# Two heads on the two halves of TensorE, and the causal mask inside VectorE's maximum

## What is computed

```python
q, k, v = (heads(wq, bq), heads(wk, bk), heads(wv, bv))      # 16 heads of 8
q, k = _apply_rope(q, cos, sin), _apply_rope(k, cos, sin)
att = jnp.einsum('bhtd,bhsd->bhts', q, k) * scale
att = jax.nn.softmax(jnp.where(causal, att, -inf), axis=-1)
y = jnp.einsum('bhts,bhsd->bhtd', att, v)
...
scores = jnp.einsum('bhid,bhjd->bhij', q * scale, k)          # the mixture, 8 heads of 64
probs = jax.nn.softmax(scores, axis=-1)
```

## The kernel before

| slot | pass 1 | pass 2 | values of |
|---|---|---|---|
| 6, 7 | A groups 0, 1 | F groups 2, 3 | F groups 1, 2 |
| 0, 1 | A groups 2, 3 | A groups 0, 1 | F group 3, A group 0 |
| 2, 3 | F groups 0, 1 | A groups 2, 3 | A groups 1, 2 |
| 4, 5 | F groups 2, 3 | F groups 0, 1 | A group 3, F group 0 |

## Time and profile before

### The profile page before, as it was taken

One profiled execution on the slowest core, in us unless ns is written; L12 is line 12 of the kernel. 1 busy time (PEld: TensorE's weight loads), 2 busy tenths in 40 slices (PEclk: granted clock), 3 DMA queues, 4 the chain that ended last, 5 costly groups with the idle time before them and its releaser, 6 DMA issues.

```text
span 2072.6 us, 32651 instructions
## 1 busy us (share of the span) xinstructions
PE 1816.3 (88%) x11328; PEld 881.0 (43%) x11328; DVE 1580.1 (76%) x2934; ACT 1273.3 (61%) x2803; POOL 1047.0 (51%) x1124
## 2 busy tenths in 40 slices
PE   1658999989999898989999998999999899998775
PEld 0223443535444353535444453544435354443332
DVE  4538787888878788788888888887878888787461
ACT  0335757576675757566675756667575766758461
POOL 1223556363645646374655636465563636455433
PEclk8879999999999999999999999999999999999986
DMA  3231203112121302113120211213021121200000
GB/s 97 48 36 32 37 29 43 35 26 30 37 37 42 36 30 33 23 37 36 42 37 30 40 33 27 33 39 37 29 44 35 26 29 37 36 17 14 11 1 6
DMA packets 87617, 68.71 MB, mean 33 GB/s; under 512 B 10720, under 2 KB 83104, under 8 KB 87328
## 3 DMA queue, kind: packets, MB, share of 16 engines
q1 hardware_dynamic: 87456, 66.62, 17.5%
HBM read 32.51 MB, written 10.49 MB: 21 GB/s over the span
## 4 chain that ended last, share of the span: by engine, by line
PE 64%; DVE 13%; ACT 10%; POOL 6%; DMA 3%; issue 3%; SPq 0%; POOLq 0%; DVEq 0%; ACTq 0%; PEldq 0%
PE Y L463 11%; PE M L556 5%; POOL Z L1069 5%; PE S2a L428 5%; ACT Pq L683 5%; PE S1c L404 5%; PE S2b L428 4%; DVE nmaxF L848 4%; PE M L593 3%; PE S1b L404 3%; PE M L514 3%; PE M L489 3%; DMA Ks<-parts 3%; DVE ztmp L930 3%; PE Y L454 2%
## 5 line engine op out<-in xcount | busy, mean ns | idle before, releaser
L1069 POOL TENSOR_TENSOR Z<-Z,ztmp 128x1280 f32<-128x1280 f32 x112 | 324.5, 2897 | 327.9 <-DVE ztmp L958 326.8
L1036 POOL TENSOR_SCALAR_AFFINE_SELECT PT<-PT 128x256 f32<-128x256 f32 (+1 forms) x640 | 254.5, 409 | 386.6 <-ACT PT L668 383.5
L1060 POOL TENSOR_TENSOR Vf<-Vf,ztmp 128x512 f32<-128x512 f32 x256 | 349.0, 1363 | 102.2 <-DVE ztmp L930 93.6
L668 ACT ACTIVATE PT<-S2a 128x512 f32<-128x512 f32 x320 | 191.6, 599 | 170.6 <-PE S2a L422 166.2
L463 PE MATMUL Y<-PT,Vf 128*64 128x512 f32 x1024 | 274.8, 617 | 0.0
L672 ACT ACTIVATE PT<-S2a 128x512 f32<-128x512 f32 x256 | 153.6, 600 | 158.5 <-PE S2a L428 155.7
L930 DVE TENSOR_TENSOR ztmp<-xv,wv_s 128x512 f32<-128x512 f32 x256 | 238.0, 930 | 2.8 <-POOL Z L1069 2.8
L404 PE MATMUL S1c<-Kf,Qf 64*128 64x512 f32 x352 | 203.6, 659 | 36.2 <-ACT Pq L683 32.2
L404 PE MATMUL S1a<-Kf,Qf 64*128 64x512 f32 x352 | 204.5, 662 | 20.6 <-ACT Pq L683 20.6
L668 ACT ACTIVATE PT<-S2b 128x512 f32<-128x512 f32 x320 | 191.5, 598 | 26.3 <-PE S2b L422 26.0
L404 PE MATMUL S1b<-Kf,Qf 64*128 64x512 f32 x320 | 182.8, 652 | 9.5 <-ACT Pq L683 9.5
(11 more groups left out here) (108 smaller groups left out, 3760.7 us busy)
## 6 DMA issues: line engine op xcount, KB each, us to landing
Qs<-parts SPq DMA_DIRECT2D x96, 128.0 KB
Ks<-parts SPq DMA_DIRECT2D x96, 128.0 KB
tab_s<-in_tab SPq DMA_DIRECT2D x16, 512.0 KB, 4.5
xr<-out_x SPq DMA_DIRECT2D x32, 256.0 KB, 2.9
out_x<-res SPq DMA_DIRECT2D x32, 256.0 KB, 2.2
wa_s<-in_wa SPq DMA_DIRECT2D x16, 320.0 KB, 3.1
xl<-out_x SPq DMA_DIRECT2D x16, 256.0 KB, 3.0
out_x<-in_x SPq DMA_DIRECT2D x8, 256.0 KB, 4.4
```

The lines of the kernel that those rows point to most:

```text
L668: nc.scalar.activation(PT[:, slot % 2, b, :], t[:, :], ACT.Exp, scale=SCALE_A).then_inc(exps_done.sem, 1)
L1036: last = nc.gpsimd.affine_select(out=v, in_=v, compare_op=ALU.is_ge, fill=0.0, base=0, pattern=pattern, channel_multiplier=-1)
L1060: nc.gpsimd.tensor_tensor(Vf[:, i, :, :], Vf[:, i, :, :], vtmp[:, n % VBUF, :, :], ALU.add).then_inc(v_acc.sem, 1)
L1069: nc.gpsimd.tensor_tensor(Z[:, :, :, :], Z[:, :, :, :], ztmp[:, hh % 2, :, :, :], ALU.add).then_inc(z_acc.sem, 1)
```

## The change

1. **Layout.** Qs and Ks are [128, 8, 512] in place of [98, 16, 512]: even heads lie in rows 0 to 63, odd heads in rows 64 to 127. A head's contraction takes 48 rows (`ROWS_P1`) and, with the two rows of maxima, 50. (The 48 rows are the six products of parts; the zero rows are left out.) The weights' columns and the tables are laid out on the host so that even heads come out in partitions 0 to 63.
2. **Pairs.** The banks are ordered so that bank b (b even) and bank b+1 hold the same segments of an even head and its odd neighbour. Pass 1 and pass 2 issue both banks at once, at even steps; the first waits until both banks are free. Of both, all matmuls of the even head come first in the program, then those of the odd one.
3. **Mask.** The 16 mask matmuls of a group are gone. VectorE takes each maximum by `tensor_tensor_reduce`: the PSUM segment plus `maskw` (zeros, and -1e30 above the diagonal in its last 128 columns), written back in place, with the maximum in an accumulator. Each of the 16 segments has its own instruction, and each becomes two on the engine: the pass over the segment, and one that writes the accumulator out.
4. **Around it.** Split and negation of the maxima are two small instructions as before. The spreading DMAs are 24 of 64 KB in place of 12 of 128 KB; the rows of maxima go as two DMAs, of two rows each. The memsets at the start cover 2048 words in place of 4096 for Qs and Ks.

```diff
-    ROWS_P1 = 96
+    ROWS_P1 = NSP * DA
     ROWS_P2 = ROWS_P1 + 2
+    HALF = 64
...
+    for h0 in range(0, GA, 2):
+        BANKS_A1 += [[(h, 3, 0)] for h in (h0, h0 + 1)] + [[(h, 2, 0), (h, 0, 384)] for h in (h0, h0 + 1)]
+        BANKS_A2 += [[(h, 0, 0)] for h in (h0, h0 + 1)] + [[(h, 1, 0), (h, 3, 384)] for h in (h0, h0 + 1)]
+    BANKS_A1 += [[(h, 1, 0), (h + 2, 1, 256)] for h in (0, 1)]
+    BANKS_A2 += [[(h, 2, 0), (h + 2, 2, 256)] for h in (0, 1)]
...
                         for r in range(NSP):
-                            sp.dma_start(dst[DA * r:DA * r + DA, :, :],
-                                         parts[:, qk, order[r], :]).then_inc(scattered.sem, 16)
+                            for lo in (0, HALF):
+                                sp.dma_start(dst[lo + DA * r:lo + DA * r + DA, :, :],
+                                             parts[lo:lo + HALF, qk, order[r], :]).then_inc(scattered.sem, 16)
...
-                    pe.wait_ge(*s1_free(j, (n if group < SA else n + 1) - len(S1)))
+                    pe.wait_ge(*s1_free(j, n + 1 - len(S1)))
                     if group < SA:
-                        for h, qt, col in BANKS_A1[b]:
-                            hh, keys = GA * group + h, (qt + 1) * P
-                            nc.tensor.matmul(t[:, col:col + keys], Qs[0:ROWS_P1, hh, qt * P:keys],
-                                             Ks[0:ROWS_P1, hh, 0:keys], start=True, stop=False)
-                            last = nc.tensor.matmul(t[:, col + qt * P:col + keys], identb[:, :], maskb[:, :],
-                                                    start=False, stop=True)
-                        last.then_inc(s1_filled.sem, 1)
+                        for i in range(2):
+                            for h, qt, col in BANKS_A1[b + i]:
+                                hh, keys, r = GA * group + h, (qt + 1) * P, HALF * (h % 2)
+                                last = nc.tensor.matmul(S1[(n - 1 + i) % len(S1)][:, col:col + keys],
+                                                        Qs[r:r + ROWS_P1, hh // 2, qt * P:keys],
+                                                        Ks[r:r + ROWS_P1, hh // 2, 0:keys], start=True, stop=True)
+                            last.then_inc(s1_filled.sem, 1)
...
-                    pe.wait_ge(exps_done.sem, exps_done.at(j, n - len(S2)))
+                    pe.wait_ge(exps_done.sem, exps_done.at(j, (n + 1 if slot < SA else n) - len(S2)))
...
+                        for h, qt, col in BANKS_A1[b]:
+                            keys = (qt + 1) * P
+                            last = nc.vector.tensor_tensor_reduce(
+                                t[:, col:col + keys], t[:, col:col + keys], maskw[:, T - keys:T], 1.0, -3.0e38,
+                                ALU.add, ALU.max, maxA[:, h % 2, GA // 2 * group + h // 2, qt:qt + 1])
                         last.then_inc(s1_read.sem, 1)
```

85 lines of the change are left out of this document (38 added, 47 removed).

## The result

The changed kernel takes 2086.45 us, median of 6 runs (2082.94 to 2088.36), against 2074.64 for the kernel before on the same chip. The ratio is 1.0052, with a 95% interval of 1.0040 to 1.0064. It is slower by 11.8 us; the forecast was 2117 us, 43 more. The profiled execution has a span of 2081.2 us.

A forecast was written before the change was run, and what follows sets the result against it. TensorE and VectorE were taken as near full together in slots 6, 7, 0 and 1, the change loading VectorE. +2.7 us a turn over 15 turns (+40.5) and +3 at the ends on 2074.4 gave 2117 us, range 2050 to 2185.

The forecast's parts named there:

- what the accumulator costs: VectorE, pass 1 maxima: 0.12 us for each of 16 segments, making a group 2.0 us longer; called the deciding term.
- the prediction's formula: VectorE: an instruction occupies the engine for its elements at 0.96 GHz and 0.067 us more.
- rival A: VectorE's accumulator is cheap and TensorE's gain is seen: same or faster, 2014 us at no cost; chance 0.26.
- the point from which the forecast turns: Accumulator price on VectorE, about 0.055 us per segment, at which the forecast changes between slower and faster.
- TensorE's saving there is worth nothing: Slots 0 and 1: VectorE sets the pace, so TensorE's 2.2 to 3.0 us saved a slot bring nothing.
- the second bank's 0.85 us to fill the next: Pass 1 pairs: TensorE fills the next in about 0.5 us while VectorE reads the second bank; no wait booked.
- TensorE's busy time: Profile after, whole span: TensorE's busy time down by over 100 us.
- 0.1 us for a change of shape: TensorE: going into or out of the half-array shape costs about 0.1 us each, read from the F pairs.
- forecast for the memsets: Start of the kernel: memsets of Qs and Ks halve, -3.5 us, with 0.4 taken back by the new one for `maskw`.
- rival C: Spreading DMAs cost by number, not bytes: 24 take 46 us, +16 us a turn, about 2360 us; chance 0.02.
- rival D: TensorE's halves do not run side by side for bf16 with 48 rows: 2140 us; chance 0.03.
- near the ideal 1.07 and not 1.48: TensorE, five pairs of banks: 1.07 us if halves never wait for one another, 1.48 in strict program order.

The follow-up runs named there:

- before_mask_on_vector: The kernel before with the mask matmuls taken out and the accumulating maximum with the mask on VectorE, no pairs: 2086.78 us, 1.0038.
- pairs_no_mask: The changed kernel with a plain tensor_reduce in place of the accumulating maximum, leaving the causal mask out of pass 1: 2085.70 us, 1.0038 against the kernel before.
- pairs_own_wait: The changed kernel with each bank of a pass 1 pair waited for separately, not both at the start: 2093.52 us, 1.0073 against the kernel before.
- pairs_pass2_alone: The changed kernel with pass 1 bank by bank on the halves and pass 2 still in pairs: 2132.85 us, 1.0262 against the kernel before.
- before_no_mask: The kernel before without its mask matmuls, VectorE as it was: 2059.29 us, 0.9935, with executions in two groups.
- pairs_pass1_alone: The changed kernel with pass 2 bank by bank and pass 1 still in pairs: 2107.22 us, 1.0136 against the kernel before.
- groups23_in_pairs: The kernel before with group 0 masked on VectorE, groups 2 and 3 on the halves in pairs with 64-row mask matmuls: 2067.92 us, 0.9947.
- before_masks_divided: The kernel before with groups 0 and 1 masked on VectorE, 2 and 3 on TensorE, no pairs: 2084.95 us, 0.9997, executions in two groups.
- before_mask0_on_vector: The kernel before with group 0 alone masked on VectorE, the other groups on TensorE: 2080.16 us, 1.0005.
- group3_in_pairs: The kernel before with group 0 masked on VectorE and group 3 alone on the halves in pairs with 64-row mask matmuls: 2067.73 us, 0.9948.

## Why the prediction was right or wrong

**The sum.** Forecast +2.7 us a turn. Measured -0.67 undisturbed, and +0.67 with the fall that comes in every turn. Slower came true, but not by the mechanism that I gave. By slots, from the table and the sum above:

| slots | forecast | undisturbed | with the fall |
|---|---|---|---|
| 0 + 1 | +3.2 | -0.42 | +0.64 |
| 6 + 7 | +0.6 | +0.71 | +0.70 |
| 2 + 3 | -1.1 | -1.23 | -0.94 |
| 4 + 5 | 0 | +0.27 | +0.26 |

**The step that failed first: what the accumulator costs.** I took 0.12 us a segment, with ends at 0 and 0.26, by the smallest VectorE instruction. VectorE's timeline in slot 0, with the read-outs:

```profile
997.46 0.70 DVE L847 CUSTOM_DVE_ANT_0 S1a<-S1a,maskw 128x512 f32<-128x512 f32 x1
998.08 0.14 DVE L847 DVE_READ_ACCUMULATOR2_ANT maxA<- 128x1 f32 x1
998.08 0.73 DVE L847 CUSTOM_DVE_ANT_0 S1b<-S1b,maskw 128x512 f32<-128x512 f32 x1
998.72 0.14 DVE L847 DVE_READ_ACCUMULATOR2_ANT maxA<- 128x1 f32 x1
```

The read-out lasts 0.14 us but starts together with the next main instruction; it takes no turn of its own. Two starts of 512 are 0.62 to 0.64 apart, where the reduction had 0.60; for 384, 256 and 128 the steps are 0.48 to 0.51, 0.38 and 0.25, for 0.467, 0.333 and 0.20 by the prediction's formula. That is some 0.04 a segment in the mean, a third of what I took. The prediction named this as what would speak for rival A ("the write-out's start within the main instruction's drain"), and set the point from which the forecast turns at 0.055. By the prediction's own two points, -3.8 us a turn at a price of 0 and 0 at 0.055, a price of 0.04 makes about -1.0 a turn (an estimate); measured is -0.67 undisturbed. So the sign of the forecast hung on this term. Rival A was nearer on the price, and its time (2014) wrong all the same, by the pairs and the clock below.

**The second: what TensorE's saving is worth in slots 0 and 1.** Undisturbed they are 10.01 and 12.98, for 10.39 and 13.02 before, though VectorE has about 0.8 us more of work in each group. In slot 0 "TensorE's saving there is worth nothing" was wrong: before, TensorE was busy for all of its 10.39 us and VectorE for 9.63. The wrong border of the earlier trace rows hid how full both were: it gave slot 0 0.7 us too much, and with it the 1.8 us of idle VectorE in slots 0 and 1, which are 1.04.

**Third: slots 6 and 7.** The forecast of +0.6 is close to the +0.71 measured, but by luck. The same mask on VectorE without pairs (before_mask_on_vector) makes the two slots 0.80 shorter; with the pairs and the halves they are 1.50 longer than that, and for the pairs I booked nothing. Slot 7 alone is 1.15 longer than before. Of this the accumulator is 0.43 (pairs_no_mask: 15.95 for 16.38), and with the same mask on VectorE and no pairs the slot is 15.20. So 0.7 to 1.2 comes with the pairs of pass 1. TensorE's timeline in slot 7, and VectorE's:

```profile
988.48 0.60 PE L471 MATMUL Y<-PT,Vf 128*64 128x512 f32 x2
990.71 0.33 PE L397 MATMUL S1c<-Ks,Qs 48*128 48x384 bf16 x1 [1.63 <-DVE maxA L847]
```
```profile
988.23 1.48 DVE L964 TENSOR_TENSOR ztmp<-M,wz 128x1280 f32<-128x1280 f32 x1
...
995.22 0.43 DVE L847 CUSTOM_DVE_ANT_0 S1b<-S1b,maskw 128x256 f32<-128x256 f32 x1 [2.39 <-PE S1c L397]
```

S1c had been free since before VectorE's mixing product. The pair waits for S1a too, which VectorE reads behind that product, and pass 2 and the F projections are queued behind the pair. VectorE later runs dry, for 2.39 us, while TensorE works through them. The prediction said that the pair "has the second bank's 0.85 us to fill the next"; it overlooked that a product of 1.48 us can stand between the two banks of a pair. Waits of TensorE's weight loads for `maxA` come to 271 us in all:

```profile
PEld S1c L397 <- DVE maxA L847: 118.6, 95, 2.5
...
PEld S1a L397 <- DVE maxA L847: 83.5, 81, 2.5
...
PEld S1b L397 <- DVE maxA L847: 69.0, 66, 2.8
```

Dividing the wait (pairs_own_wait) did not help in slot 7: the second half of the pair still stands ahead of the rest of the queue. Without pairs of pass 1 (pairs_pass2_alone) the slot is 0.53 shorter. How much of the 0.7 to 1.2 is the wait and how much the changes of shape is not settled.

**Fourth, not in the prediction at all: the clock.** With less of its own work TensorE waits 1.90 us in slot 1. The clock falls there, and the fall costs 1.07 in slot 1 and 0.3 in slot 2. This turns a gain of 0.67 into a loss of 0.67. The pairs are not needed for it: before_mask_on_vector and before_no_mask have a fall in every turn too. The earlier trace rows showed a clock of 1.00 in every slot of the full turns, and I took that for granted. The row 66:82 among them, clock 0.84 where TensorE had gaps, was the hint. The Trainium skill, "TensorE: Matmul & The Clock Gate", section HAM oscillation, describes a loop in which every round begins slow because TensorE waited in the round before. The traces agree that a loop can pay for the clock in every turn: it is at 0.50 once a turn, and the price is 1.38 us in the same program.

**What was right.** Slots 2 and 3 together (-1.1 forecast, -1.23 undisturbed), which pairs_pass1_alone and groups23_in_pairs give to the pairs of pass 2, though slot 3, expected to gain little, has 0.56 of it; TensorE's busy time; 0.1 us for a change of shape; and the DMAs: rival C did not come, each 12 of the 24 spreads are issued in 8.1 us, and the last ones land some 8 us before slot 6. The halves do work side by side, so rival D fell too. TensorE's timeline in slot 0:

```profile
997.03 0.39 PE L397 MATMUL S1a<-Ks,Qs 48*128 48x512 bf16 x1
997.04 0.39 PE L397 MATMUL S1b<-Ks,Qs 48*128 48x512 bf16 x1
997.26 0.38 PE L428 MATMUL S2a<-Qs,Ks 50*128 50x512 bf16 x1
...
999.17 0.33 PE L397 MATMUL S1c<-Ks,Qs 48*128 48x384 bf16 x1
999.18 0.33 PE L397 MATMUL S1a<-Ks,Qs 48*128 48x384 bf16 x1
999.34 0.22 PE L397 MATMUL S1c<-Ks,Qs 48*128 48x128 bf16 x1
999.35 0.22 PE L397 MATMUL S1a<-Ks,Qs 48*128 48x128 bf16 x1
```

Two banks of 512 pass in 0.23 us, and so do two of 384 and 128. In the program both matmuls of S1c stand ahead of both of S1a, and yet 384 starts on both halves before 128 on either. So a start on one half doesn't wait for the program's order on the other, and five pairs take 1.15 us, near the ideal 1.07 and not 1.48. The rule that the prediction cites from the Trainium skill, "TensorE: Matmul & The Clock Gate", under what overlaps and what doesn't, that matmuls start in strict program order, doesn't hold between halves here; the measurement decides.

**The ends.** The first pass 1 begins 8.3 us earlier (58.42 for 66.70): 3.6 ahead of the first spread, about as forecast for the memsets, and 4.7 because the spreads are through sooner, where I had booked +1. The waits for `Ks` in the two chains, before and changed:

```profile
48.37 18.29 DMA Ks<-parts
```
```profile
51.18 7.20 DMA Ks<-parts
```

By the first mark of `F out` 1.9 of the 8.3 are left, at a mean clock of 0.83 between for 0.92 before.

## What to carry to other kernels

Before work is taken off TensorE, look at what it does just ahead and behind in the profile's granted clock: where it is left to wait in a loop (1.90 us here), the clock can fall in every turn, and the fall can cost more than the work saved. Idle repeats in that gap, into a bank that is written anyway, are a cheap test. In groups23_in_pairs they gained 12 us; in the changed kernel the fall only moved to the next gap, so read all slots.

Running two heads side by side pays where the neighbours have the same shape and nothing else stands between the two banks (slots 2 and 3); where another engine puts a long instruction between them, the pair waits for it and everything queued behind waits too.

## What the runs showed of the hardware

Turns of 119.45 to 119.47 us come back in eight kernels (the changed one, pairs_no_mask, before_mask_on_vector, before_no_mask, before_masks_divided in its slower group, before_mask0_on_vector, group3_in_pairs, groups23_in_pairs), whose undisturbed turns, where seen, are 118.08, 118.12 and 118.30. The fall comes at the same place in each of these turns. In pairs_no_mask slot 1 swallowed to 0.1 us what other slots had won. So while the loop is in this state small gains and losses can't be seen in the time. In the changed kernel the falls begin 119.47 us apart, twelve times in a row from 417.6 to 1851.2, while the turns between them vary from 119.29 to 119.81: the falls keep their distance and the turn follows. Why it is this length is left open.

A VectorE instruction with an accumulator writes it out by a second one of 0.14 us that costs the engine no slot; the main one costs about 0.04 us more than the plain reduction.

With the same bytes in twice the transfers, the time from the first issued spread to the first pass 1 fell from 27.6 to 22.9 us at the start, where TensorE waits for it. In a full turn the landings took nearly as long as before (about 21 us for 23), and no run changes the size of the transfers alone.
